# First and last gathers of a fused graph network: rows of three bfloat16 parts, summed by three products, instead of float32 rows

## What is computed

```python
# layer 0, first gather
agg = jax.ops.segment_sum(h[src], dst, num_segments=N)
z = (1.0 + eps_gin) * h + agg          # then two products with batch norms
# layer 3, last gathers: a turn by target, a turn by source
msgs = xl[src]
agg = jax.ops.segment_sum(msgs, dst, num_segments=num_nodes)   # and with src and dst swapped
```

## Time and profile before

| | |
|---|---|
| time, median of 3 runs (lowest to highest) | 7637.69 us (7620.69 to 7654.07) |
| span of the profiled execution | 7527.2 us |
| what lies around the span, against the median | 110.5 us |
| PE / PEld / DVE / ACT / POOL busy | 71% / 41% / 42% / 7% / 63% |
| `step_tables` | 0 to 58 us |
| `first_gather` | 58 to 1350 us |
| `attend_close` | 4597 to 4803 us |
| `last_gathers`, first turn / second turn | 4806 to 6060 us / 6060 to 7311 us |

### The profile page before, as it was taken

One profiled execution on the slowest core, in us unless ns is written; L12 is line 12 of the kernel. 1 busy time (PEld: TensorE's weight loads), 2 busy tenths in 40 slices (PEclk: granted clock), 3 DMA queues, 4 the chain that ended last, 5 costly groups with the idle time before them and its releaser, 6 DMA issues. The chain is left out here.

```text
span 7527.2 us, 81611 instructions
## 1 busy us (share of the span) xinstructions
PE 5373.7 (71%) x17807; PEld 3065.0 (41%) x17807; DVE 3160.7 (42%) x6956; ACT 545.2 (7%) x1542; POOL 4732.4 (63%) x4778
## 2 busy tenths in 40 slices
PE   5666777638765556636566687788888888888887
PEld 2333333525332223324444575433433344444444
DVE  2222444528655556674444567511111123333317
ACT  0000000324000000010000001100000000000004
POOL 5666665664666666677677404766666666666665
PEclk8777777969767777767778899865555588888869
DMA  4444433331688888846667675433333333333445
GB/s 137 133 134 130 124 123 121 128 100 66 214 256 256 265 262 268 266 134 210 210 217 226 205 191 148 126 89 89 90 89 87 89 111 119 119 119 119 123 101 191
DMA packets 693161, 1164.20 MB, mean 155 GB/s; under 512 B 104128, under 2 KB 490285, under 8 KB 692614
## 3 DMA queue, kind: packets, MB, share of 16 engines
q0 software_dynamic: 224288, 633.55, 28.9%
q1 hardware_dynamic: 468344, 525.21, 21.9%
q10 hardware_dynamic: 110, 0.23, 0.0%
HBM read 870.83 MB, written 287.77 MB: 154 GB/s over the span
## 5 line engine op out<-in xcount | busy, mean ns | idle before, releaser
L2126 PE MATMUL l_sums<-big 128*128 (+1 forms) x3520 | 1701.9, 578 | 349.1 <-issue 135.1
L195 DVE TENSOR_TENSOR big<-iota_row,dst_tab 128x512 f32<-128x512 f32 x660 | 458.4, 695 | 2171.3 <-PE l_sums L2126 712.1
L1280 POOL DMA_INDIRECT bin_rows<-staging,place_tab x832 | 979.6, 1177 | 337.4 <-issue 249.1
L1166 POOL DMA_INDIRECT big<-kv_rows,idx_tab x880 | 832.0, 945 | 503.0 <-issue 241.1
L578 POOL DMA_INDIRECT big<-in_x,big x832 | 826.6, 994 | 483.6 <-SPq L148 237.7
L2083 POOL DMA_INDIRECT big<-x_rows,place_tab x880 | 882.3, 1003 | 394.9 <-issue 241.7
L2083 POOL DMA_INDIRECT big<-x_rows,idx_tab x832 | 817.2, 982 | 426.7 <-issue 226.6
L1220 PE MATMUL es_q<-big 128*128 x1760 | 720.9, 536 | 450.3 <-issue 343.3
L2126 PEld LDWEIGHTS l_sums<-big 128*128 128x128 f32 x3520 | 765.2, 259 | 502.0 <-issue 473.7
L612 PE MATMUL l_sums<-big 128*128 x1760 | 723.0, 543 | 331.9 <-issue 235.8
L1504 PE MATMUL ws_sums<-big 128*128 128x264 f32 x1760 | 546.1, 474 | 321.2 <-DVE big L1524 170.9
(11 more groups left out here) (297 smaller groups left out, 5187.4 us busy)
## 6 DMA issues: line engine op xcount, KB each, us to landing
v_edge<-big SPq DMA_DIRECT2D x880, 128.0 KB
big<-v_edge SPq DMA_DIRECT2D x220, 512.0 KB
bin_rows<-big SPq DMA_DIRECT2D x110, 520.0 KB
sims<-bin_rows SPq DMA_DIRECT2D x110, 520.0 KB
staging<-in_edges SPq DMA_DIRECT2D x104, 520.0 KB
gate_rows<-big SPq DMA_DIRECT2D x49, 512.0 KB
big<-gate_rows SPq DMA_DIRECT2D x49, 512.0 KB
big<-kv_rows,idx_tab POOLq DMA_INDIRECT x880
```

Source lines behind the costliest of these rows:

```text
L195: return dve.tensor_tensor(out, rows, columns.unsqueeze(2).to_broadcast([P, QUAD, P]), ALU.is_equal)
L1166: pool.indirect_dma_start(ring[:, u, :], None, k.kv_rows, bass.IndirectOffsetOnAxis(ap=k.idx[:, s:s + 1], axis=0)).then_inc(s_row[u], 16)
L1280: pool.indirect_dma_start(k.bin_rows, bass.IndirectOffsetOnAxis(ap=k.place[:, c:c + 1], axis=0), k.staging[:, g % 2, j, :], None).then_inc ...
L2126: pe.matmul(sums[:, bank_of(node[u] + turn, D)], onehot[:, u % HALF, :], flat[:, bass.ds(at, D)], start=False, stop=True, skip_group_check ...
```

## The change

The features are stored as three bfloat16 parts (high part, middle part, rest), 768 numbers in a row instead of 256 float32: 1536 bytes instead of 1024. The gathers read these rows; each step multiplies the one-hot matrix, now bfloat16 too, with the three parts one after the other, into the same bank. For the first gather the parts are made in `step_tables`: the load of the features is cut into 7 groups of 7 windows, and for each group ACT rounds to the high part, DVE subtracts it, ACT rounds to the middle part, DVE subtracts that to the low part, and SP stores the group. For the last gathers the same four operations and a store are added to each window of `attend_close`. `push` and its product are gone. Counts, the ring's depth of 16, the relays on SP and the ACT side stay as they are, and the float32 rows are still stored.

```diff
+PARTS = 3
+GROUP_W = 7
+SPLITS = NW // GROUP_W
+SLOTS = 4
+RW = PARTS * D + 2
...
-def push(pe, k, spare):
-    ones = k.ones.bitcast(BF16)
-    pe.matmul(spare, ones[:, 0:1], ones[:, 0:1], start=True, stop=True)
...
-            sp.dma_start(k.X, x_rows.rearrange("(w p) d -> p w d", p=P)).then_inc(s_x, 16)
+            for g in range(SPLITS):
+                sp.dma_start(k.X[:, windows(g), :],
+                             x_rows.rearrange("(w p) d -> p w d", p=P)[:, windows(g), :]).then_inc(s_in[g], 16)
+            def send_parts(g):
+                sp.wait_ge(s_low, g + 1)
+                sp.dma_start(k.x_parts.rearrange("(w p) d -> p w d", p=P)[:, windows(g), :],
+                             parts[:, g % SLOTS, :, :]).then_inc(s_sent[g % SLOTS], 16)
...
+            send_parts(0)
+            send_parts(1)
             sp.wait_ge(s_lasts, 4)
             sp.dma_start(k.last_row, k.lasts).then_inc(s_x, 16)
+            for g in range(2, SPLITS):
+                send_parts(g)
...
+        @block.scalar
+        def _(act):
+            def high_part(g):
+                act.wait_ge(s_in[g], 16)
+                if g >= SLOTS:
+                    act.wait_ge(s_sent[g % SLOTS], 16 * (g // SLOTS))
+                act.copy(parts[:, g % SLOTS, :, 0:D], k.X[:, windows(g), :]).then_inc(s_high, 1)
+            def middle_part(g):
+                act.wait_ge(s_rest, g + 1)
+                act.copy(parts[:, g % SLOTS, :, D:2 * D], rest[:, g % 2, :, :]).then_inc(s_middle, 1)
+            high_part(0)
+            high_part(1)
+            for g in range(SPLITS):
+                middle_part(g)
+                if g + 2 < SPLITS:
+                    high_part(g + 2)
...
+            def take_high(g):
+                dve.wait_ge(s_high, g + 1)
+                if g >= 2:
+                    dve.wait_ge(s_low, g - 1)
+                dve.tensor_tensor(rest[:, g % 2, :, :], k.X[:, windows(g), :], parts[:, g % SLOTS, :, 0:D],
+                                  ALU.subtract).then_inc(s_rest, 1)
+            def low_part(g):
+                dve.wait_ge(s_middle, g + 1)
+                dve.tensor_tensor(parts[:, g % SLOTS, :, 2 * D:], rest[:, g % 2, :, :], parts[:, g % SLOTS, :, D:2 * D],
+                                  ALU.subtract).then_inc(s_low, 1)
+            take_high(0)
+            take_high(1)
+            low_part(0)
+            low_part(1)
...
+            take_high(2)
+            for g in range(3, SPLITS):
+                take_high(g)
+                low_part(g - 1)
+            low_part(SPLITS - 1)
...
-        ring = room.take([P, U, D + 1])
+        ring = room.take([P, U, RW], BF16)
         flat = ring.rearrange("p u d -> p (u d)")
-        onehot = room.take([P, HALF, P])
+        onehot = room.take([P, HALF, P], BF16)
...
-                pool.indirect_dma_start(ring[:, u, 0:D], None, table, bass.IndirectOffsetOnAxis(
+                pool.indirect_dma_start(ring[:, u, 0:PARTS * D], None, table, bass.IndirectOffsetOnAxis(
...
-                pe.matmul(sums[:, bank_of(node[u], width)], onehot[:, u % HALF, :],
-                          flat[:, bass.ds(slot_of(s, node[u], D + 1), width)],
-                          start=False, stop=True, skip_group_check=True).then_inc(s_sum, 1)
+                at = slot_of(s, node[u], RW)
+                for n, columns in enumerate((D, D, width)):
+                    ins = pe.matmul(sums[:, bank_of(node[u], columns)], onehot[:, u % HALF, :],
+                                    flat[:, bass.ds(at + n * D, columns)], start=False, stop=True, skip_group_check=True)
+                ins.then_inc(s_sum, 1)
...
+            def send_parts(w, slot, nodes):
+                sp.wait_ge(s_low, w + 1)
+                sp.dma_start(k.x3_parts[bass.ds(w * P, P), :], parts[:, slot, :]).then_inc(s_parts[slot], 16)
+            over(sp, (load, 0), (send, 6), (send_parts, 8))
...
+            def high_part(w, slot, nodes):
+                act.wait_ge(s_new, w + 1)
+                if not early(w, S):
+                    act.wait_ge(s_parts[slot], turns(w, slot, 1))
+                act.copy(parts[:, slot, 0:D], x[:, node_window(w)]).then_inc(s_high, 1)
+            def middle_part(w, slot, nodes):
+                act.wait_ge(s_rest, w + 1)
+                act.copy(parts[:, slot, D:2 * D], rest[:, slot, :]).then_inc(s_middle, 1)
+            over(act, (second_root, 3), (first_root, 2), (copy_turned, 0), (high_part, 5), (middle_part, 6))
...
+            def take_high(w, slot, nodes):
+                dve.wait_ge(s_high, w + 1)
+                dve.tensor_tensor(rest[:, slot, :], x[:, node_window(w)], parts[:, slot, 0:D],
+                                  ALU.subtract).then_inc(s_rest, 1)
+            def low_part(w, slot, nodes):
+                dve.wait_ge(s_middle, w + 1)
+                dve.tensor_tensor(parts[:, slot, 2 * D:], rest[:, slot, :], parts[:, slot, D:2 * D],
+                                  ALU.subtract).then_inc(s_low, 1)
             over(dve, (count, 0), (first_inverse, 3), (divide, 0), (twice, 3), (add, 2), (add_terms, 3),
                  (measure_first, 2), (second_inverse, 4), (measure_second, 3), (first_moments, 2), (close, 4),
-                 (second_moments, 3))
+                 (second_moments, 3), (take_high, 6), (low_part, 7))
...
-        spare = psum(nc, ctx, "l3_spare", [1, BANK])
...
-                pool.indirect_dma_start(ring[:, u, :], None, k.x3_rows, bass.IndirectOffsetOnAxis(
+                pool.indirect_dma_start(ring[:, u, :], None, k.x3_parts, bass.IndirectOffsetOnAxis(
...
-                pe.matmul(sums[:, bank_of(node[u] + turn, D)], onehot[:, u % HALF, :], flat[:, bass.ds(at, D)],
-                          start=False, stop=True, skip_group_check=True).then_inc(s_sum, 1)
-                push(pe, k, spare[:, 0:1])
+                for n in range(PARTS):
+                    ins = pe.matmul(sums[:, bank_of(node[u] + turn, D)], onehot[:, u % HALF, :], flat[:, bass.ds(at + n * D, D)],
+                                    start=False, stop=True, skip_group_check=True)
+                ins.then_inc(s_sum, 1)
...
-        first_gather(nc, k, a["x"])
+        first_gather(nc, k, k.x_parts)
```

More of the change, by code:

```diff
@@ L1634, in attend_close @@
         part = sets.take([P, S, D])
+        parts = sets.take([P, S, PARTS * D], BF16)
+        rest = room.take([P, S, D])
         tps = [psum(nc, ctx, f"ac_t{i}", [P, 512]) for i in range(2)]
@@ L1647, in attend_close @@
         s_gate = sems(nc, k, *(f"nt_gate{i}" for i in range(S)))
+        s_high, s_rest, s_middle, s_low = sems(nc, k, *(f"sp_{n}" for n in ("high", "rest", "middle", "low")))
+        s_parts = sems(nc, k, *(f"sp_sent{i}" for i in range(S)))
         block = ctx.enter_context(nc.Block())
@@ L2121, in _ @@
                     chunk_ready(pe, t, node[u], s_here)
-                at = u * D if turn else slot_of(t, node[u], D)
+                at = u * PARTS * D if turn else slot_of(t, node[u], PARTS * D)
                 if t % QUAD == 0:
```

25 lines of the change are left out of this document (19 added, 6 removed).

## The result

The changed kernel takes 7823.62 us (median of 4 runs, 7797.97 to 7829.53) against 7632.96 us for the kernel before (4 runs, 7620.69 to 7654.07): ratio 1.0247, 95% interval 1.0218 to 1.0276. It is slower by 191 us; 7785 was forecast, 147 us slower.

A forecast was written before the change was run, and what follows sets the result against it. POOL was taken to wait for PE in all three gather stages, its own pace only a tenth below. The terms 167 + 5 - 70 + 40 + 5 = +147 us on 7637.7 gave 7785 us, the forecast's own range 7680 to 8000.

The forecast's parts named there:

- Sequencer: PE, first gather and first turn: its sequencer paces steps; two more instructions at 0.16 us each give 1.04 us a step.
- holes: PE, first gather and first turn: "issue" stretches of 1.0 to 2.3 us, sequencer held up, growing by a third with instructions.
- Engine: PE's engine, gather steps: three bfloat16 products cost 0.95 of one float32 product; a float32 step takes 0.95 us at half clock.
- First gather: First gather stage: steps +167 us, holes +89, waits for landings and one-hot gone, -89; sum +167 us.
- First turn: First turn of the last gathers: steps -120 us, holes beginning to show +216, waits gone -91; sum +5 us.
- Second turn: Second turn of the last gathers: PE only gains, capped by POOL's 151 us of waits; half taken, -70 us.
- attend_close: In attend_close, two more DVE subtractions on the path of each of 49 windows, 0.40 us each: +40 us (32 to 69).
- tables: In step_tables, 30 us of subtractions against 27.5 us of DVE idle time, plus seven stores: +5 us, 0 to +25.
- The sum's base: Whole kernel: the profiled execution was taken as 7527.2 + 110.5 = 7637.7 us, the median itself.
- Rival A: First gather and first turn: POOL's pace decides, PE needs less than before; about 7400 us, chance 0.32.
- Rival B: Second turn: PE's clock falls to 0.5, the stage grows by 281 us; about 8135 us, chance 0.06.
- C, a balance: Whole kernel: first gather's loss returns in first turn, or buffers set the pace; within 38 us of now, chance 0.08.

The follow-up runs named there:

- six_addresses: The changed kernel with each part's product cut into two of 128 columns, each with its own ring address; 7266.33 us, ratio 1.0908 to the kernel before.
- One_address: The changed kernel with all three products of a step reading the ring at one address; 6695.16 us, ratio 1.0064 to the kernel before.
- By_step_parts: The changed kernel with buffers and steps one to one in first gather and first turn, without relay; 6804.83 us, ratio 1.0226 to the kernel before.

## Why the prediction was right, and where not

Sign and total held (7785 for 7824, inside 7680 to 8000), the parts less so. That the total is near is in part luck: the first gather came out 129 us below its forecast, the first turn 138 us above, the second 75 us above. Of the signs named for being right, the steps and the window turns are there. PE's "issue" in the first gather (283 us) and POOL's wait for the relay (277 us) stay below the 300 us asked for, and PE's waits for landings did not vanish.

- **Sequencer, right.** The step came out at 0.99 to 1.04 us, on both kinds of chip, and six_addresses shows the mechanism by itself. A further address costs 0.12 to 0.15 us; I had taken 0.16. One_address with eight less two is at the 0.72 of the earlier trace rows. That the holes are the sequencer being held up was right too: its instructions take 0.7 us each there.
- **Engine, too dear.** I took three bfloat16 products at 0.95 of a float32 one, from single products of 392 columns, whose duration holds more than their columns. I also divided a stretch of 3.79 us by its four steps, though it ends with the tail of the last product: the steps start 0.86 us apart, not 0.95. Three bfloat16 products take the engine 0.62 to 0.64 us at half clock, three quarters of the float32 one. It did not matter much, since the sequencer was slower.
- **First gather, +167 forecast, +38 measured.** The step that failed: the stage's other parts were left at full length beside a slower step. Take the distances between the starts of successive steps. Those under 1.5 us grew from 0.79 to 0.97 us on average, by 0.17 where +0.19 was forecast, which makes about +153 us for 880 steps. What the longer ones have beyond an ordinary step, holes, waits and other products, fell by 112 us, from 594 to 482, where the forecast let it stay (+89 - 89). PE's other products explain part of it. The 210 or so steps that follow such products came 2.26 us after the one before on average, and now 1.95, though a step costs the sequencer more: while the engine works on the others, the sequencer goes on with the next step. The waits for landings and one-hot did not go either (70 + 19 us before, 122 + 10 now).
- **First turn, +5 forecast, +143 measured.** The ordinary step did what was forecast, from 1.18 to 1.04 us, -122 us. The term mis-sized is what the holes cost once the engine has no backlog: the distances over 1.5 us had 196 us beyond an ordinary step before (190 forecast as 98 + 92) and have 464 now, where 314 was forecast. Their number went from 122 to 233, though the sequencer's slow instructions only went from 248 to 282. This fits hold-ups that a step of 1.25 us on the engine had covered and that now show, which is the forecast's reasoning with a larger number; no run on that chip tests it. That the slow instructions grow by a third with the instructions is not borne out: by 23% in the first gather, by 14% here.
- **Second turn, -70 forecast, +5 measured: a wait that was misread.** PE did get faster, and POOL's wait for it merely changed its name (18 + 141 us for 84 + 67). The gain went into DVE's queue. Before, DVE sat idle at L2005 for 113 us and at one more place (what waits for what: us in total, times, longest):

```profile
DVE big L2011 <- DMA v_edge<-big: 55.6, 11, 6.4
```

After:

```profile
PE l_sums L2224 <- DVE big L195: 370.8, 57, 10.5
...
DVE big L2103 <- DMA v_edge<-big: 218.3, 35, 11.3
...
DVE big L2109 <- DMA v_edge<-big: 106.1, 17, 9.9
```

I called this a wait for edge rows, and that is wrong. Edge rows (`v_edge`) are stored by an earlier stage; no DMA of the second turn touches them. In the program L2103 waits for two things, PE's product and the store of the last window's gates, and L2109 only for PE's product. In the turn below DVE had passed the wait for the store at 6632.2 us, and the last product of L2137 that it needs ends by 6635.3. DVE starts 6.5 us later:

```profile
6634.27 1.02 PE L2137 MATMUL gp_g<-sims,big 128*128 128x512 f32 x2
...
6641.82 0.69 DVE L2103 TENSOR_TENSOR big<-gp_g,big 128x512 f32<-128x512 f32 x1 [8.97 <-DMA v_edge<-big]
```

The changed kernel on a later chip, where DVE starts 0.04 us after the product:

```profile
5479.70 1.02 PE L2137 MATMUL gp_g<-sims,big 128*128 128x512 f32 x2
...
5480.77 0.69 DVE L2103 TENSOR_TENSOR big<-gp_g,big 128x512 f32<-128x512 f32 x1 [3.06 <-PE gp_g L2137]
```

Over the 98 such operations of the turn, DVE starts 194 us later in all than its own queue, the store and PE's product would let it before the change, and 266 us later after it. On the later chip it is 4 us for both kernels. So on the first chip DVE, or the signal that reaches it, is held up as well. The one-hot matrices are queued behind these operations on the same engine, and PE waits 371 us for them, where it was 95 us. I had named the row and let it stay; it took the whole gain. Why DVE's late starts grew by 72 us is open.
- **attend_close, +40 forecast, +42 measured; tables +5, +12**, inside their bounds. In the tables I asked whether DVE had room, which it had, and did not ask what its work does to POOL's gathers beside it.
- **The sum's base.** "What lies around the span" was a misreading: in all later runs the time is within 3 us of the span. The 110.5 us were a difference between executions. It did no harm, since the sum was made from differences.
- **Rival A** asked where POOL's pace decides: below 1.23 us a step with holes. That is the state of the later chips, for the kernel before too, so nothing is gained there either and 7400 has no counterpart. **Rival B**: the clock in the second turn fell from 0.83 to 0.75, not to 0.5. The gates' products did not suffer: 224 + 120 + 44 = 387 us for 419. On the rule of the Trainium skill (TensorE: Matmul & The Clock Gate, Why this matters for your kernels) that idle gaps bring back half clock the trace agrees as far as 0.71 became 0.54 and 0.57 became 0.51 in the stages full of idle stretches. But idle time alone does not order the stages. In the kernel before PE was busy for 85% of the first turn and 84% of the second, at 0.57 and 0.83; I had called the first one full of idle stretches, and it was not. And without push the first turn had more idle time (796 us busy for 991 of 1053) at a higher clock (0.72 for 0.62). The same page's 107 ns for a load (LDWEIGHTS) is met: the changed kernel's loads take 103 to 105 ns (median), beside the products.
- **C, a balance**: on chips without holes the change is at +0.56%, just outside the band.

No version beat both kernels by more than 0.5%. The quickest on the later chips was the kernel before without push. By_step_parts takes most of the sequencer's work away and may be the better one where PE's sequencer has holes, but no run reached such a chip, so this was not tried there.

## What to carry to other kernels

Replacing one float32 product by three bfloat16 ones of the same width saved engine time here (0.86 to 0.64 us a step at half clock), but each further product whose address depends on a register cost the engine's sequencer 0.12 to 0.15 us; count both and compare with the pace of what feeds them. Where a sequencer sets the pace, products beside it are in part hidden under it, and engine time that is saved has nowhere to go. Check a wait's name against the program before building on it: a DMA that does not run in the stage cannot end a wait there. Before optimising an engine, look at who sets the pace on more than one chip: the gathers were at 1.3 us each everywhere, and only one chip made PE slower than they.

## What was not expected

The same program takes 7633 us on one chip and 6656 to 6666 us in four jobs on others. The durations of single operations agree (a gather has a median of 946 ns on both, the float32 steps are busy for 714 and 702 us). What differs is how long the sequencers take: over 0.3 us for 444 of PE's 9238 instructions that wait for nothing, and for 219 of 1656 on SP, which carries the relay; none on the later chip. DVE starts late after PE's products as well. The stages are longer on the first chip: first gather 1293 against 1081 us from first to last gather, first turn 1234 against 1053, second turn 1276 against 1136; the last stage, after the gathers, takes 214 and 216 us. In the second turn PE's own slow instructions are few (none of 864 before the change, 12 of 909 after), and the late starts are DVE's.

What holds the sequencers up on that chip is open. The traces of that chip also hold only 40% of the updates of semaphores that the later ones have. And in a hole, to go by the order of the records, an address is recorded 0.66 us after the product that uses it has started (for the three products from 5613.82 to 5615.25 us: at 5614.49, 5615.20 and 5615.91), where in an ordinary step it is recorded before. So the writing of the trace itself may hold the sequencers up there; a setting of the chip may too, and no run tells them apart. There the change costs 2.5%, elsewhere 0.56%, and PE takes POOL's place as the bound.
